# Moving the diagonal key blocks to ScalarE and the probability copies off VectorE in a row-pipelined attention stage

## The chip, the cores and the metric

The kernel runs on one core of a Trainium2 chip. The metric is the device time of the whole program in microseconds, median of several executions. Five engines work in parallel, each on an instruction stream of its own that it executes strictly in order: TensorE (PE: matmuls and transposes), VectorE (DVE), ScalarE (ACT), GpSimd (POOL) and SyncE (SP, which issues transfers). They meet only in semaphores: an instruction may add to one when it is done, and an engine may wait until one has reached a number. Everything behind a waiting instruction on the same engine waits with it.

## The reference

Eight layers on x of shape (8, 128, 256): four attentions, each followed by a feed-forward part. The change touches the second pair. What is computed there, cut to what matters:

```python
x = x + L1_xattn(layernorm(x), ctx)      # 16 heads of 16, T = 128 rows against 128 keys, 8 batch rows
    q = rms_norm(x @ Wq + bq, gq);  k = rms_norm(ctx @ Wk_img + bk_img, gk_img);  v = ctx @ Wv_img + bv_img
    out = softmax(q k^T / 4) v  @ Wo + bo
x = x + L1_ffn(layernorm(x))             # 256 -> 1024 -> 256, 4-bit fake-quantised
    h = relu(x_q @ W1_q^T + b1_q);  h_q = clip(round(h / s2), 0, 15) * s2;  out = h_q @ W2_q^T + b2_q
```

Every batch row (128 x 256) is independent of the others here, which is what the kernel pipelines over.

## The kernel before

The program is one long hand-written schedule. Each engine's part of a stage is a Python function, and the stage of the change is `s23_pe`, `s23_act`, `s23_dve` and `s23_pool` (lines 1331 to 1753). The order in which an engine's calls are written is its order on the chip; nothing reorders it.

A batch row's attention is done in two halves h = 2n and 2n + 1 of eight heads each. `WINDOWS` runs w from -4 to 15, and every engine makes its share of window w before that of w + 1. With k, odd = divmod(w, 2), the even and the odd window of "row k" hold, beside the softmax work of half w, pieces of other batch rows: the projections and the RMS norm of row k + 2, the residual and layer norm of row k - 1, and the feed-forward of rows k - 2 and k - 3. The functions that the prediction follows, with the line of the instruction:

- PE: `scores(w + 1)` L1376, `turn_probs(w)` L1383 (transposes the probabilities), then in an even window `output` L1406, `down(k - 3)` L1442, `project_context(k + 2)` L1340, `project_rows(k + 2)` L1346, `up(k - 2, 0)` L1434, and in an odd one `turn_rows` L1419, `turn(k + 2)` L1361, `up(k - 2, 1)` L1434; last in each window `weigh(w)` L1398 (probabilities times values).
- ACT: `copy_probs` L1485, `exps` L1493, `squares` L1504 (sums of squares for the RMS norm), `copy_rows` L1518, `copy_qk` L1512, `relu` L1527.
- DVE: `maxima` L1590, `normalise` L1581, `divide` L1603 and L1607, `copy_probs` L1597, `add` L1620, `feed` L1637 and L1640, the layer-norm statistics L126 to L130, `apply` L134, `bias` L1564, `values` L1571, `quantise` L1626 and L1630.
- POOL: `ln_rsqrt` L139, `rms` L1686 and L1689, `bias` L1702, `diagonal` L1696, `quantise` L1706 to L1712.

`diagonal` builds c_kb, in which the keys of each head stand in rows of their own with zeros elsewhere, by multiplying the 128 x 128 key block with the four columns of a 0/1 mask `hm`; `scores` needs it. The transposed probabilities of one half lie in two PSUM banks of 512 columns; ACT copies the first bank and DVE the second, each with a semaphore (`c_PT`, `c_PTv`), and `weigh` waits for both. After the last `weigh` PE goes on with the next layer's projections (L1919), issued behind it in the same stream.

Of the kernel before, what the change touches and what calls it, by code (L numbers as in the profile page):

```python
# [25 lines left out]
ALU = mybir.AluOpType  # L26
# [5 lines left out]
KD = D // 128  # L32
# [39 lines left out]
def build(nc, x, ctx, ctxT, mask, maskT, kvmask, a_wqT, a_wkT, a_wvT, a_bq, a_bk, a_bv, a_sel,  # L72
# [5 lines left out]
    with ex:  # L78
# [1252 lines left out]
        def s23_pe(pe):  # L1331
# [32 lines left out]
            def scores(h):  # L1364
                n, c = divmod(h, 2)
                pe.wait_ge(c_qkT, n + 1)
                pe.wait_ge(c_kbd, h + 1)
                if h == 1:
                    pe.wait_ge(c_qkT, 2)
                    pe.wait_ge(c_v, 2)  # L1370
                if h >= 2:
                    pe.wait_ge(c_PT, h - 1)
                    pe.wait_ge(c_PTv, h - 1)
                for i in range(2):
                    half = slice(64 * i, 64 * i + 64)
                    t = pe.matmul(P[:, 2 + 2 * c + i, :], c_qT[n % 2][half, c, :], c_kb[n % 2][half, c], start=True,  # L1376
                                  stop=True)
                t.then_inc(c_s, 1)
# [8 lines left out]
            def weigh(h):  # L1387
                n, c = divmod(h, 2)
                pe.wait_ge(c_PT, h + 1)
                pe.wait_ge(c_PTv, h + 1)  # L1390
                pe.wait_ge(c_v, n + 1)
                if c == 0 and n > 0:
                    pe.wait_ge(c_x, n)
                for what in range(2):
                    for i in range(2):
                        for r in range(4):
                            j = 2 * r + i
                            t = pe.matmul(P[32 * r:32 * r + 32, 6, c * D + what * T:c * D + what * T + T],  # L1398
                                          c_one[:, i, :] if what else c_vp[n % 3][:, 8 * c + j, :],
                                          c_pt[h % 2][:, j, :], start=(i == 0), stop=(i == 1))  # L1400
                t.then_inc(c_pv, 1)
# [47 lines left out]
            for w in WINDOWS:  # L1449
                k, odd = divmod(w, 2)  # L1450
                if 0 <= w + 1 < HALVES:
                    scores(w + 1)
                if 0 <= w < HALVES:
                    turn_probs(w)
                if not odd:
                    if 0 <= k - 1 < B:
                        output(k - 1)
                    if 0 <= k - 3 < B:
                        down(k - 3)
                    if 2 <= k + 2 < B:  # L1460
                        project_context(k + 2)
                        project_rows(k + 2)
                    elif k == -2:
                        project_rows(0)
                else:
                    if 0 <= k - 1 < B:
                        turn_rows(k, 1)
                    if 0 <= k + 2 < B:
                        turn(k + 2)
                    if k == -2:  # L1470
                        project_rows(1)
                if 0 <= k - 2 < B:
                    up(k - 2, odd)
                if 0 <= w < HALVES:
                    weigh(w)
                if 1 <= w + 5 < B:
                    turn_routed(w + 5)
            return output, turn_rows, up, down

        def s23_act(act):  # L1480
            def copy_probs(h):
                act.wait_ge(c_t, h + 1)
                if h >= 2:
                    act.wait_ge(c_pv, h - 1)
                act.activation(c_pt[h % 2][:, 0:4, :].rearrange("p j t -> p (j t)"), P[:, 2 + 2 * (h % 2), :],  # L1485
                               ACT.Copy).then_inc(c_PT, 1)

            def exps(h):
                act.wait_ge(c_mx, h + 1)
# [17 lines left out]
            def copy_qk(n):  # L1507
                act.wait_ge(c_tr, n + 1)
                if n >= 2:
                    act.wait_ge(c_s, 2 * n - 2)  # L1510
                    act.wait_ge(c_kbd, 2 * n - 2)
                act.activation(c_qT[n % 2].rearrange("p j t -> p (j t)"), P[:, QK_BANK[n], :], ACT.Copy).then_inc(c_qkT, 1)  # L1512

            def copy_rows(k, bank):
                act.wait_ge(tb_pe, TURNED[k])
# [22 lines left out]
            for w in WINDOWS:  # L1538
                k, odd = divmod(w, 2)
                if 0 <= w < HALVES:  # L1540
                    copy_probs(w)
                if 0 <= w + 1 < HALVES:
                    exps(w + 1)
                if not odd:
                    if 0 <= k + 2 < B:
                        squares(k + 2)
                else:
                    if 0 <= k - 1 < B:
                        copy_rows(k, 1)
                    if 0 <= k + 2 < B:  # L1550
                        copy_qk(k + 2)
                if 0 <= k - 2 < B:
                    relu(k - 2, odd)
                if 1 <= w + 5 < B:
                    copy_routed(w + 5)
            return copy_rows, relu

        def s23_dve(dve):
# [26 lines left out]
            def maxima(h):  # L1585
                dve.wait_ge(c_s, h + 1)
                if h >= 2:
# [1 line left out]
                bank = 2 + 2 * (h % 2)  # L1589
                dve.tensor_reduce(c_m[h % 2], P[:, bank:bank + 2, :].rearrange("p a (j t) -> p (a j) t", t=T), AX.X,  # L1590
                                  ALU.max, negate=True).then_inc(c_mx, 1)

            def copy_probs(h):
                dve.wait_ge(c_t, h + 1)
                if h >= 2:
                    dve.wait_ge(c_pv, h - 1)
                dve.tensor_copy(c_pt[h % 2][:, 4:8, :].rearrange("p j t -> p (j t)"),  # L1597
                                P[:, 3 + 2 * (h % 2), :]).then_inc(c_PTv, 1)

            def divide(h):  # L1600
                n, c = divmod(h, 2)
# [46 lines left out]
            for w in WINDOWS:  # L1648
                k, odd = divmod(w, 2)
                if 0 <= w + 1 < HALVES:  # L1650
                    maxima(w + 1)
                if odd and 0 <= k + 2 < B:
                    normalise(k + 2)
                if odd and 0 <= w - 1 < HALVES:
                    divide(w - 1)
                if 0 <= w < HALVES:
                    copy_probs(w)
                if not odd:
                    if 0 <= k - 1 < B:
                        add(k - 1)  # L1660
                    if 0 <= k - 3 < B:
                        feed(k - 3)
                    if 0 <= k - 1 < B:
                        apply("attend", k - 1)
                    if 0 <= k - 3 < B:
                        apply("feed", k - 3)
                    if 0 <= k + 2 < B:
                        bias(k + 2)
                        values(k + 2)
                else:  # L1670
                    if 0 <= k - 2 < B:
                        quantise(k - 2, 0)
                    if 0 <= w < HALVES:
                        divide(w)
                    if 0 <= k - 2 < B:
                        quantise(k - 2, 1)
                if 2 <= w + 6 < B:
                    routed_row(dve, w + 6)
            return add, quantise, feed, apply

        def s23_pool(pool):
            def rms(n):
# [4 lines left out]
                    c_ve, 1)  # L1687
                pool.wait_ge(c_ve, n + 1)
                pool.tensor_tensor(c_rst[:, n % 2, :], c_vet[:, n % 2, :], mhalf[:, 0:2], ALU.pow).then_inc(c_rs, 1)  # L1689

            def diagonal(n):
                pool.wait_ge(c_qkT, n + 1)
                for c in range(KD):
                    if n >= 2:
                        pool.wait_ge(c_s, 2 * n - 3 + c)
                    pool.tensor_tensor(c_kb[n % 2][:, c], c_qT[n % 2][:, 2 + c:3 + c, :].broadcast_to([128, 4, T]),  # L1696
                                       hm.rearrange("p (j a) -> p j a", a=1).broadcast_to([128, 4, T]),
                                       ALU.mult).then_inc(c_kbd, 1)

            def bias(n):  # L1700
                pool.wait_ge(xn_ready, 2 * B + n + 1)
                pool.tensor_tensor(X[:, n, :], X[:, n, :], cbo, ALU.add).then_inc(c_cb, 1)  # L1702
# [26 lines left out]
            for w in WINDOWS:  # L1729
                k, odd = divmod(w, 2)  # L1730
                if odd and 2 <= w + 6 < B:
                    routed(w + 6)
                if not odd:
                    if 0 <= k - 1 < B:
                        ln_rsqrt(pool, LN_FIRST + 2 * B + LN23["attend", k - 1], LN23["attend", k - 1] % 2)
                    if 0 <= k - 3 < B:
                        ln_rsqrt(pool, LN_FIRST + 2 * B + LN23["feed", k - 3], LN23["feed", k - 3] % 2)
                    if 0 <= k + 2 < B:
                        rms(k + 2)
                    if 2 <= w + 6 < B:  # L1740
                        routed(w + 6)
                else:
                    if 0 <= k < B:
                        bias(k)
                    if 0 <= k + 2 < B:
                        diagonal(k + 2)
                    if 0 <= k - 1 < B:
                        quantise(k - 1)
            for what in (("attend", B - 1), ("feed", B - 3)):
# [1403 lines left out]
```

## Time and profile before

| | |
|---|---|
| time, median of 3 runs | 1213.58 us (1206.4 to 1214.52) |
| the profiled execution: its own time | 1215.49 us |
| its span in the trace | 1213.5 us |
| busy: PE / DVE / ACT / POOL | 1058.6 / 717.7 / 502.6 / 319.9 us |
| the stage of the change, first `exps` to last `weigh` | 441.53 to 563.00 us, 121.47 us |
| busy in it: PE / DVE / ACT / POOL | 98.99 / 96.24 / 73.45 / 54.59 us |

Times inside the program are microseconds from the start of the span. In the row lists below a line reads: start, length, engine, source line, operation, tensors written and read, count. Neighbouring instructions of the same kind are merged into one line; the brackets give idle time ahead of it and what ended that. Because instructions of one engine overlap a little, the distance from one start to the next is the price of an instruction in a full queue, and its length is what somebody who waits for its result sees. "issue" means that the releaser of a wait is not visible.

### The profile page before, as it was taken

The numbers are of one execution on the slowest core, as the hardware profiler recorded it, in microseconds if no ns is written. First come the engines' busy times: TensorE is split into PE (matmuls) and PEld (weight loads), VectorE is DVE, ScalarE is ACT, GpSimd is POOL, SyncE is SP. The second block draws the span as 40 slices with busy tenths as digits, with TensorE's granted clock in tenths as the row PEclk, the third lists the DMA queues.
The fourth block names the chain that finished last, engine by engine and source line by source line (L and its number), as shares of the span: only waits on it lengthen the run. The fifth ranks groups of instructions, "written<-read, shape, count | busy, mean of one in ns | idle before, by whom it ended". The sixth has DMA issues, their size and how long they took to land.

```text
span 1213.5 us, 20040 instructions
## 1 busy us (share of the span) xinstructions
PE 1058.6 (87%) x6826; PEld 803.0 (66%) x6826; DVE 717.7 (59%) x1700; ACT 502.6 (41%) x1785; POOL 319.9 (26%) x440
## 2 busy tenths in 40 slices
PE   6898788699999868878999999999789999996694
PEld 3665555489999745656878777776556666664472
DVE  5576775711222276887656565566677777775544
ACT  2255557233333144665433334243445555554120
POOL 6252331112332233553100000001212222220572
PEclk9899999689999968989999999999999999999797
DMA  6764442689888406100111101122000000000795
GB/s 194 268 209 143 142 133 81 240 314 331 317 329 321 141 26 227 52 1 31 36 55 36 36 1 36 35 88 88 1 1 5 5 5 6 6 5 13 223 312 180
DMA packets 85218, 141.72 MB, mean 117 GB/s; under 512 B 10090, under 2 KB 58490, under 8 KB 79202
## 3 DMA queue, kind: packets, MB, share of 16 engines
q1 hardware_dynamic: 71193, 116.84, 29.1%
q0 software_dynamic: 4416, 12.06, 2.9%
q10 hardware_dynamic: 9508, 11.55, 2.8%
q8 instruction: 55, 0.90, 0.3%
q14 instruction: 46, 0.37, 0.1%
HBM read 117.51 MB, written 22.72 MB: 116 GB/s over the span
## 4 chain that ended last, share of the span: by engine, by line
PE 60%; DVE 12%; DMA 9%; issue 7%; ACT 4%; SPq 4%; POOL 3%; DVEq 0%; POOLq 0%; ACTq 0%
PE P L968 6%; PE P L978 6%; PE P L1928 4%; PE P L1968 4%; PE P L2114 4%; PE P L2061 4%; DMA scr_qk<-big 3%; PE P L1919 3%; PE P L2880 2%; PE P L2067 2%; PE P L2103 2%; PE P L2089 2%; DMA big<-placed 2%; PE P L2897 1%; PE P L1940 1%
## 5 line engine op out<-in xcount | busy, mean ns | idle before, releaser
L139 POOL TENSOR_TENSOR lrs<-lve,mhalf 128x1 f32<-128x1 f32 x64 | 36.6, 572 | 328.3 <-DVE lve L130 284.2
L576 DVE TENSOR_REDUCE small<-P 128x2 f32<-128x512 f32 x128 | 84.2, 683 | 44.4 <-PE P L403 44.4
L1009 ACT ACTIVATE big<-P,big 128x128 f32<-128x128 f32 x184 | 52.4, 368 | 124.5 <-PE P L968 124.5
L2255 ACT ACTIVATE big<-P,small 128x128 f32<-128x128 f32 x128 | 45.2, 366 | 128.4 <-DVE small L2438 128.4
L656 ACT ACTIVATE big<-P 128x512 f32<-128x512 f32 x128 | 73.6, 599 | 59.0 <-PE P L423 52.0
L968 PE MATMUL P<-big 128*128 128x128 f32 x736 | 87.5, 278 | 0.6 <-DMA big<-b_w 0.5
L968 PEld LDWEIGHTS P<-big 128*128 128x128 f32 x736 | 85.6, 195 | 1.1 <-DMA big<-b_w 1.1
L1111 DVE COPY big<-P 128x256 f32<-128x256 f32 x23 | 9.8, 425 | 125.9 <-PE P L978 125.9
L978 PE MATMUL P<-big 128*128 128x256 f32 x368 | 83.1, 379 | 0.0
L271 PE MATMUL P<-CT,big 128*128 128x256 f32 (+1 forms) x224 | 69.7, 441 | 5.7 <-ACT big L248 4.4
L978 PEld LDWEIGHTS P<-big 128*128 128x128 f32 x368 | 68.2, 190 | 8.4
L403 PE MATMUL P<-big 90*128 90x256 bf16 x256 | 51.1, 282 | 13.8 <-DVE small L576 12.2
L1919 PE MATMUL P<-XNT,big 128*128 128x128 f32 x512 | 62.6, 275 | 0.0
L2114 PE MATMUL P<-big 128*128 128x256 f32 x256 | 61.8, 385 | 0.4 <-DVE big L2635 0.4
L2356 ACT ACTIVATE big<-P 128x512 f32<-128x512 f32 x32 | 19.1, 597 | 102.5 <-PE P L2067 102.5
L2061 PE MATMUL P<-big,XNT 128*128 128x512 f32 x128 | 60.4, 594 | 1.1 <-DVE big L2579 1.1
L1968 PE MATMUL P<-big 128*128 128x256 f32 x256 | 60.6, 380 | 0.0
L1928 PE MATMUL P<-big,CT 128*128 128x512 f32 x128 | 60.1, 592 | 0.0
L1919 PEld LDWEIGHTS P<-XNT,big 128*128 128x128 f32 x512 | 59.7, 192 | 0.2 <-issue 0.2
L2347 ACT ACTIVATE big<-P,small 128x128 f32<-128x128 f32 x128 | 56.7, 459 | 5.2 <-DVE small L2624 5.2
L2429 DVE COPY big<-P 128x512 f32<-128x512 f32 x32 | 22.1, 691 | 60.5 <-PE P L1928 60.4
L1152 POOL DMA_INDIRECT moe_y<-big x23 | 25.0, 1089 | 122.3 <-DVE big L1111 122.3
(387 smaller groups left out, 2530.8 us busy)
## 6 DMA issues: line engine op xcount, KB each, us to landing
big<-b_w SPq DMA_DIRECT2D x23, 1028.0 KB
big<-b_w SPq DMA_DIRECT2D x23, 1024.0 KB
big<-scr_qk SPq DMA_DIRECT2D x96, 96.0 KB
big<-keys_t SPq DMA_DIRECT2D x8, 1024.0 KB, 6.4
big<-i_wgu SPq DMA_DIRECT2D x23, 352.0 KB
keys_t<-XNT ACTq DMA_DIRECT2D x24, 256.0 KB, 2.1
big<-moe_y SPq DMA_DIRECT2D x16, 256.0 KB, 4.3
big<-i_wd SPq DMA_DIRECT2D x23, 176.0 KB
```

Source lines behind the costliest of these rows:

```text
L271: t = pe.matmul(P[:, key_bank(p), lo:hi], k_wts[:, g, k, 128 * j:128 * j + 128], CT[:, k, 512 * r + lo:512 * r + hi], start=(k == 0), stop ...
L576: dve.tensor_reduce(negM[:, h, :], P[:, h % 2, :].rearrange("p (c s) -> p c s", c=2), AX.X, ALU.max, negate=True).then_inc(a_max, 1)
L656: act.activation(ER[:, g % 8], P[:, second_bank(i), :].rearrange("p (c t) -> p c t", c=2), ACT.Exp).then_inc(a_e, 1)
L968: m = pe.matmul(P[:, 2 * (j % 2) + f // 4, f % 4 * 128:f % 4 * 128 + 128], w1x[j % 3][:, k * F0 + f * 128:k * F0 + f * 128 + 128], xgT[j % ...
L978: m = pe.matmul(P[:, 6 + j % 2, 0:D], hT[j % 2][:, f, :], w2x[j % 3][:, f, :], start=(f == 0), stop=(f == FC - 1))
L1009: act.activation(hT[j % 2][:, f, :], P[:, 2 * (j % 2) + f // 4, f % 4 * 128:f % 4 * 128 + 128], ACT.Gelu_apprx_tanh, bias=w1x[j % 3][:, 2 ...
L1919: t = pe.matmul(P[:, 0, j * T:j * T + T], e_wqs[:, g, k, j * 128:j * 128 + 128], XNT[:, k, b * T:b * T + T], start=(k == 0), stop=(k == KD ...
L1928: t = pe.matmul(P[:, 2, :], CT[:, k, b * T:b * T + T], e_wvs[:, g, k, :], start=(k == 0), stop=(k == KD - 1))
L1968: t = pe.matmul(P[:, 7, 0:D], e_o[:, j, :], e_wos[:, 4 * g + j, :], start=(g == 0 and j == 0), stop=(g == 3 and j == 3))
L2061: t = pe.matmul(P[:, 0, :], XNT[:, k, b * T:b * T + T], h_wqs[:, g, k, :], start=(k == 0), stop=(k == KD - 1))
L2114: t = pe.matmul(P[:, 7, 0:D], h_o[:, j, :], h_wos[:, 4 * g + j, :], start=(g == 0 and j == 0), stop=(g == 3 and j == 3))
L2347: t = act.activation(h_pr[m % 2][:, j, :], P[:, 4 - 2 * (m % 2), j * T:j * T + T], ACT.Exp, bias=h_bi[m % 2][:, j:j + 1], scale=h_rq[:, m ...
```

## The change

1. `diagonal` moves from POOL to ACT: where POOL used one 128 x 512 multiplication for each half (two for each batch row), ACT uses four copies of 128 x 128 with a per-partition scale `hm[:, j:j + 1]` (eight for each batch row). It stands right behind `copy_qk`, which now goes ahead of `copy_rows`.
2. ACT's `copy_probs` copies both PSUM banks in one instruction of 1024 columns, and DVE's is gone. `weigh(h)` now waits for `c_o >= h`, that is for `divide(h - 1)`, where it waited for `c_PTv`.
3. DVE's `bias` stands ahead of the two `apply` calls, where it stood behind them.
4. ACT's `relu(k - 2, 0)` stands ahead of `squares(k + 2)`, where it stood behind; `relu(k - 2, 1)` stays behind the copies of its window.
5. PE's `up(k - 2, 1)` stands ahead of `turn(k + 2)`, where it stood behind.

The diff, cut to its core:

```diff
 PE      if h >= 2:
             pe.wait_ge(c_PT, h - 1)
-            pe.wait_ge(c_PTv, h - 1)
...
         def weigh(h):
             pe.wait_ge(c_PT, h + 1)
-            pe.wait_ge(c_PTv, h + 1)
+            if h > 0:
+                pe.wait_ge(c_o, h)
...
             if 0 <= k - 1 < B:
                 turn_rows(k, 1)
+            if 0 <= k - 2 < B:
+                up(k - 2, 1)
             if 0 <= k + 2 < B:
                 turn(k + 2)
...
-        if 0 <= k - 2 < B:
-            up(k - 2, odd)
+        if not odd and 0 <= k - 2 < B:
+            up(k - 2, 0)
...
 ACT     copy_probs(h):
-        act.activation(c_pt[h % 2][:, 0:4, :].rearrange("p j t -> p (j t)"), P[:, 2 + 2 * (h % 2), :],
-                       ACT.Copy).then_inc(c_PT, 1)
+        bank = 2 + 2 * (h % 2)
+        act.activation(c_pt[h % 2].rearrange("p j t -> p (j t)"),
+                       P[:, bank:bank + 2, :].rearrange("p a n -> p (a n)"), ACT.Copy).then_inc(c_PT, 1)
...
+    def diagonal(n):
+        act.wait_ge(c_qkT, n + 1)
+        for c in range(KD):
+            if n >= 2:
+                act.wait_ge(c_s, 2 * n - 3 + c)
+            for j in range(4):
+                t = act.activation(c_kb[n % 2][:, c, j, :], c_qT[n % 2][:, 2 + c, :], ACT.Copy,
+                                   scale=hm[:, j:j + 1])
+            t.then_inc(c_kbd, 1)
...
         if not odd:
+            if 0 <= k - 2 < B:
+                relu(k - 2, 0)
             if 0 <= k + 2 < B:
                 squares(k + 2)
         else:
+            if 0 <= k + 2 < B:
+                copy_qk(k + 2)
+                diagonal(k + 2)
             if 0 <= k - 1 < B:
                 copy_rows(k, 1)
-            if 0 <= k + 2 < B:
-                copy_qk(k + 2)
-        if 0 <= k - 2 < B:
-            relu(k - 2, odd)
+            if 0 <= k - 2 < B:
+                relu(k - 2, 1)
...
 DVE     (copy_probs(h) and its call are gone)
         if not odd:
             if 0 <= k - 1 < B:
                 add(k - 1)
             if 0 <= k - 3 < B:
                 feed(k - 3)
+            if 0 <= k + 2 < B:
+                bias(k + 2)
             if 0 <= k - 1 < B:
                 apply("attend", k - 1)
             if 0 <= k - 3 < B:
                 apply("feed", k - 3)
             if 0 <= k + 2 < B:
-                bias(k + 2)
                 values(k + 2)
...
 POOL    (diagonal(n) and its call are gone)
```

How the streams stand now. ScalarE, from the second `exps` of row 2 through row 3: L1493 is `exps`, L1504 `squares`, L1527 `relu`, L1485 `copy_probs`, L1518 `copy_rows`, L1512 `copy_qk`. Before:

```order
220 L1493 ACTIVATE big<-P,small 128x128 x8
221 L1518 ACTIVATE XNT<-P 128x2x128 x2
222 L1512 ACTIVATE big<-P 128x512
223 L1527 ACTIVATE big<-P,small 128x128 x4
224 L1485 ACTIVATE big<-P 128x512
225 L1493 ACTIVATE big<-P,small 128x128 x8
226 L1504 ACTIVATE big,small<-big 128x256 x2
227 L1527 ACTIVATE big<-P,small 128x128 x4
228 L1485 ACTIVATE big<-P 128x512
```

And ScalarE now, where L1496 is `exps`, L1515 `copy_qk`, L1523 the new `diagonal`, L1531 `copy_rows`, L1540 `relu`, L1488 `copy_probs`, L1507 `squares`:

```order
225 L1496 ACTIVATE big<-P,small 128x128 x8
226 L1515 ACTIVATE big<-P 128x512
227 L1523 ACTIVATE big<-big,small 128x128 x8
228 L1531 ACTIVATE XNT<-P 128x2x128 x2
229 L1540 ACTIVATE big<-P,small 128x128 x4
230 L1488 ACTIVATE big<-P 128x1024
231 L1496 ACTIVATE big<-P,small 128x128 x8
232 L1540 ACTIVATE big<-P,small 128x128 x4
233 L1507 ACTIVATE big,small<-big 128x256 x2
234 L1488 ACTIVATE big<-P 128x1024
```

Eleven instructions (one `copy_qk`, eight `diagonal`, two `copy_rows`) now stand between the odd window's `exps` and its `relu` where three stood, and the even window's `relu` has changed places with `squares`.

VectorE at the end of the even window of row 3, where L1637 and L1640 are `feed`, L134 the two `apply`, L1564 `bias`, L1571 `values` and L1590 the next `maxima`. Before:

```order
444 L1640 TENSOR_TENSOR X<-X,big 128x256
445 L126 BN_STATS lstat<-X 128x6
446 L128 BN_AGGR lmv<-lstat 128x2
447 L130 TENSOR_SCALAR lve<-lmv 128x1
448 L134 TENSOR_SCALAR XN<-X,lmv,lrs 128x256 x2
449 L1564 TENSOR_TENSOR big<-P,big 128x512
450 L1571 TENSOR_TENSOR big<-P,big 128x8x16 x2
```

And VectorE at that place now, where L1649 is `feed` and L1580 `bias`:

```order
437 L1649 TENSOR_TENSOR X<-X,big 128x256
438 L126 BN_STATS lstat<-X 128x6
439 L128 BN_AGGR lmv<-lstat 128x2
440 L130 TENSOR_SCALAR lve<-lmv 128x1
441 L1580 TENSOR_TENSOR big<-P,big 128x512
442 L134 TENSOR_SCALAR XN<-X,lmv,lrs 128x256 x2
```

`bias` has moved ahead of both `apply` instructions, and the copy L1597 that stood behind `maxima` and behind `divide` is gone from the stream.

## Rows read from the trace of the kernel before

**Rows 1.** Windows of core 0: length, then busy time of each engine, granted clock.
```profile
499.42:514.79 15.37, 12.71 (x139) 9.63 (x138) 13.59 (x30) 10.05 (x34) 7.97 (x10) 1.00 0.01 2
514.79:531.11 16.32, 13.53 (x135) 10.01 (x134) 13.44 (x29) 10.37 (x36) 7.97 (x10) 0.90 0.01 2
```

**Rows 2.** Timeline of VectorE, one batch row (k = 3 to k = 4).
```profile
499.42 1.21 DVE L1590 TENSOR_REDUCE small<-P 128x8 f32<-128x1024 f32 x1
501.15 1.33 DVE L1581 SCALAR_TENSOR_TENSOR big<-big,small 128x256 f32<-128x256 f32 x2 [0.52 <-POOL small L1689]
502.40 0.94 DVE L1603 RECIPROCAL big<-P 128x128 f32<-128x128 f32 x1
...
503.59 0.68 DVE L1597 COPY big<-P 128x512 f32<-128x512 f32 x1
504.19 0.42 DVE L1626 TENSOR_SCALAR big<-big 128x512 f32<-128x512 f32 x1
504.64 0.43 DVE L1630 TENSOR_SCALAR big<-big 128x512 bf16<-128x512 f32 x1
505.51 0.96 DVE L1603 RECIPROCAL big<-P 128x128 f32<-128x128 f32 x1 [0.45 <-PE P L1398]
...
506.71 0.71 DVE L1626 TENSOR_SCALAR big<-big 128x512 f32<-128x512 f32 x1
507.96 1.22 DVE L1590 TENSOR_REDUCE small<-P 128x8 f32<-128x1024 f32 x1
...
513.46 0.41 DVE L134 TENSOR_SCALAR XN<-X,lmv,lrs 128x256 f32<-128x256 f32 x1 [0.44 <-POOL lrs L139]
513.79 0.68 DVE L1564 TENSOR_TENSOR big<-P,big 128x512 f32<-128x512 f32 x1
```

**Rows 3.** Timeline of TensorE in the same batch row.
```profile
502.54 0.66 PE L1361 MATMUL P<-idf,big 128*128 128x128 f32 x4 [1.93 <-DVE big L1581]
504.37 1.08 PE L1398 MATMUL P<-big 128*32 128x128 f32 x32 [0.73 <-issue]
...
508.24 1.04 PE L1442 MATMUL P<-big 128*128 128x256 bf16 x8
509.11 1.89 PE L1340 MATMUL P<-big,CT 128*128 128x256 f32 x8
...
511.70 0.61 PE L1434 MATMUL P<-big 128*128 128x128 bf16 x8
512.25 1.08 PE L1398 MATMUL P<-big 128*32 128x128 f32 x32
...
514.32 1.09 PE L1383 MATMUL P<-idf,big 128*128 128x128 f32 x8
```

**Rows 4.** Timeline of ScalarE in the same batch row.
```profile
499.14 0.42 ACT L1504 ACTIVATE big<-big 128x256 f32<-128x256 f32 x1 [3.11 <-DVE big L1564]
...
499.96 1.48 ACT L1527 ACTIVATE big<-P,small 128x128 f32<-128x128 f32 x4
501.32 0.60 ACT L1485 ACTIVATE big<-P 128x512 f32<-128x512 f32 x1
501.80 2.19 ACT L1493 ACTIVATE big<-P,small 128x128 f32<-128x128 f32 x8
503.79 0.74 ACT L1518 ACTIVATE XNT<-P 128x256 f32<-128x256 f32 x2
504.32 0.70 ACT L1512 ACTIVATE big<-P 128x512 f32<-128x512 f32 x1
504.80 1.62 ACT L1527 ACTIVATE big<-P,small 128x128 f32<-128x128 f32 x4
```

**Rows 5.** Timeline of GpSimd in the same batch row.
```profile
505.10 2.04 POOL L1696 TENSOR_TENSOR big<-big,small 128x512 f32<-128x512 f32 x2 [3.29 <-ACT big L1512]
507.24 1.20 POOL L1706 TENSOR_SCALAR big<-XNT,small 128x256 f32<-128x256 f32 x1
```

**Rows 6.** Timeline of TensorE: the next batch row's `weigh`.
```profile
519.74 1.94 PE L1398 MATMUL P<-big 128*32 128x128 f32 x32 [0.73 <-issue]
```

More of the change, by code:

```diff
@@ L1591, in maxima @@
                                   ALU.max, negate=True).then_inc(c_mx, 1)
[L1593 to L1598, printed above, removed]
             def divide(h):
@@ L1655, in s23_dve @@
                     divide(w - 1)
-                if 0 <= w < HALVES:
-                    copy_probs(w)
                 if not odd:
@@ L1689, in rms @@
                 pool.tensor_tensor(c_rst[:, n % 2, :], c_vet[:, n % 2, :], mhalf[:, 0:2], ALU.pow).then_inc(c_rs, 1)
[L1691 to L1698, printed above, removed]
             def bias(n):
@@ L1744, in s23_pool @@
                         bias(k)
-                    if 0 <= k + 2 < B:
-                        diagonal(k + 2)
                     if 0 <= k - 1 < B:
```

## The prediction

> **What bounds the kernel now.** The table of windows comes first. One batch row takes 15.37 us at full clock and 16.32 us in the next, where the granted clock averages 0.90 [rows 1]. In those 15.37 us DVE is busy 13.59, PE 12.71, ACT 10.05 and POOL 7.97 us. No engine is full, but DVE is nearest, and busy lengths of neighbours overlap, so the timelines decide.
>
> Read VectorE's next [rows 2]. It stands still three times for another engine: 0.52 us at `normalise` for POOL's reciprocal roots, 0.45 us at the second `divide` for `weigh`, 0.44 us at `apply` for POOL. All else is its own queue. Then TensorE [rows 3]: it stands 1.93 us at `turn` for `normalise` and 0.73 us at `weigh`, whose releaser the view calls "issue". By the code it is DVE's copy: L1597 starts at 503.59 and lasts 0.68, so it ends at 504.27, and `weigh` starts at 504.37 [rows 2, 3]. So in this stage the row's time is set by DVE, with short excursions through `bias`, `squares`, `rms`, `normalise` and through `weigh`. Behind the stage PE goes on in the same stream, so what PE's last `weigh` gains or loses the kernel gains or loses.
>
> **The change part by part.** I price an instruction by the distance between starts where it sits in a full queue, and by its length where somebody waits for it; a handover between engines costs about 0.05 us.
>
> DVE's copy goes: 504.19 - 503.59 = 0.60 us, twice in a batch row, 1.20 us [rows 2]. Moving `bias` ahead of the two `apply` costs nothing on DVE and covers the 0.44 us wait, since `bias` is 0.68 us long [rows 2]. The wait that `weigh` gets in place of the removed one (`divide(h - 1)`) was already implied by DVE's order and ends 0.60 us earlier than the copy did.
>
> ACT takes the work. The eight `exps` run from 501.80 to 503.79, 0.25 us each [rows 4]. Like them a `diagonal` piece is 128 x 128 with one per-partition operand, so I take 8 x 0.25 = 2.0 us. Bounds: two per-partition operands, as in `relu`, cost (501.32 - 499.96) / 4 = 0.34 us, or 2.7 us in all; with none, a 512-column copy takes 0.48 and a 256-column one (504.32 - 503.79) / 2 = 0.265, and that line reaches 0.16 at 128 columns, or 1.3 us [rows 4]. The row nearest in shape and operands is `exps`. `diagonal` also waits for the end of `copy_qk`, so that one costs its length of 0.70 instead of 0.48. The copy of both banks costs 0.48 + 2 x 0.215 = 0.91 us on the same line, 0.43 more than half of it.
>
> A page states a price for such instructions. The Trainium skill (ScalarE: Activation LUTs, What ACT_TABLE_LOAD costs) gives 186 ns plus 0.833 ns a column, 93 ns more for each per-partition operand and 93 ns of overlap; an estimate from it is 8 x 0.293 = 2.3 us for `diagonal`, which would put the sum of this part about 1.2 us higher. The `exps` rows, at 0.25 us, lie under its figure, and I stay with them.
>
> POOL loses 2.04 us that nobody waited long for [rows 5]. That hides nothing: `scores` uses these blocks most of a batch row later. Its `quantise` now waits for the later `copy_rows`, still in time for `up` one row later.
>
> Now the placement, which I think decides. In the odd window `relu(k - 2, 1)` runs from 504.80 to 506.42 and DVE takes its result at 506.71, so it has 0.29 us to spare [rows 2, 4]. After the change `diagonal` (2.0), the longer `copy_qk` (0.22) and the wider copy (0.43) stand ahead of it: 2.65 us, less 0.29, is 2.35 us late. Behind this `relu` queue DVE's `quantise(k - 2, 1)`, the next `maxima` and `add`, and on PE `down(k - 2)` of the next window with both projections, `up`, `weigh` and `scores` behind it. With PE's late work the ACT queue is fed late, and the circle closes. Round it once, at full clock:
>
> - `relu` 1.5 and handover 0.05;
> - `quantise`, 506.71 to 507.96, 1.25 us beside GpSimd's work (0.88 alone, 504.19 to 505.07), and 0.05 [rows 2];
> - PE from the start of `down` at 508.24 through projections, `up`, `weigh`, `scores` to the end of `turn_probs` at 515.41: 7.17 us, and 0.05 [rows 3];
> - ACT: copy 0.91, `exps` 1.99, `copy_qk` 0.70, `diagonal` 2.0, `copy_rows` 0.53.
>
> That is 16.2 us, or 15.8 with the faster `quantise`, against 15.37 now: 0.5 to 0.85 us more for each round. `relu(., 1)` and `diagonal` meet in the odd windows of k = 2 to 5, so there are three rounds.
>
> What a page says bears on that 1.25. The second `quantise` takes 0.71 for the first of its two instructions while POOL's L1696 runs (505.10 to 507.14), the first one 0.42 with POOL idle [rows 2, 5]. The Trainium skill (GPSIMD Engine Reference, 8. Key points) has POOL share its SBUF interfaces with VectorE and slow two-port and two-input instructions; the trace agrees. POOL's L1696 goes, but POOL's L1706, 1.20 us, is released by `copy_rows` just ahead of `relu` and so lies beside this `quantise` again, and I expect no relief.
>
> The sum, to the path of PE's last `weigh`: rows k = 0 and 1, where no `relu` runs, gain the copy ahead of `weigh` (0.60) and up to 0.9 more from the even window's copy and the earlier `bias`, 1.2 to 3.0 for both, I take -2.0. Row 2 enters the circle: +2.35. Three rounds: +1.5 to +2.5, I take +2.0. In rows 6 and 7 there is no `diagonal`; DVE's copies leave the path (-0.6 each of four) and the wider copies enter it where ACT is late (+0.43 each), between -2.4 and +1.7, I take -0.5. Total about +2 us. The profiled execution took 1215.49 us, 2 us more than its span for what lies around it, so it would come to 1217.4. It lies 1.9 above the median, and the same sum on the median of 1213.58 gives 1215.5. With both ends of `diagonal`'s price (+-0.7 a row in four rows) and of the other terms the forecast case spans about -4 to +8, so 1209.5 to 1221.5.
>
> **The rivals.** *DVE's relief wins.* Should the odd `relu` not be late (pieces nearer 0.16 us, and ACT reaching `copy_qk` before PE's `turn` is done), the next circle runs through `normalise` 1.25, `divide` 1.19, handover 0.05, PE from `weigh` at 504.37 to the end of `up` at 512.31, 7.94, handover 0.05, `relu` 1.36, then `squares` and `rms` to `normalise` 2.0 (499.14 to 501.15) [rows 2 to 4]. That is 13.85 us, 1.5 less than now. Four rows give -6, the first two -2, the last two -1: 1204.6. For it speaks that ACT is busy only 10.05 of 15.37 us [rows 1]; against it, that its slack lies in the even window, and the additions in the odd one.
>
> *The clock.* Slower than before. PE stands 1.93 + 0.73 us in a batch row now, and that row kept full clock; the next one, with the same pauses, fell to an average of 0.90, `weigh` took 1.94 in place of 1.08 us and the row 0.95 us more [rows 1, 3, 6]. After the change PE would have a further pause, at `down`: `turn_probs` and `output` are done 3.9 us after `weigh` starts (504.37 to 508.24), but the circle releases `down` some 2.3 us after that. If that pause makes the grant fall to 1.2 GHz in each of six rows, what follows is `down`, the projections and `up`, all on the circle: 0.95 to 1.7 us a row, 6 to 10 us, on top of +2: 1221.5 to 1225.5, say 1224. It decides from about one fall in each row; the trace shows one in two.
>
> That the change doesn't do what it says is excluded by the instruction orders: all five moves are in them.
>
> **How the numbers follow.** Forecast case 0.68, 1215.5 us. DVE's relief 0.14, 1204.6. The clock 0.18, 1224. One per cent, about what a measurement of this kernel can tell from no change, is 12.1 us: 1201.5 to 1225.7. The relief case passes it less than half the time (0.06), the clock case about half the time (0.10), the forecast's own ends about 0.01 each. So 0.07 faster, 0.82 within, 0.11 slower. The range reaches from the better half of the relief case to the upper end of the clock case, 1206 to 1225.5, and leaves out about 2 in 10.
>
> **What the profile after would show.** Right: `quantise` of the odd window waiting 2 us or more for ACT's `relu`; PE waiting about as long at `down` for that `quantise`; no "issue" wait of 0.7 us at `weigh` with DVE behind it, but some wait for `divide`; `diagonal` pieces of 0.25 us from start to start; ACT busy near 14 us in each row; rows 3 to 5 at 15.8 to 16.2 us each; the first rows shorter than now. Wrong: DVE without a wait at the odd `quantise` and rows near 14 us (relief); granted clock under 0.9 over the stage (clock). The forecast would fail above all if ACT's queue has room that I don't see, if `diagonal` from SBUF costs something else than `exps` from PSUM, or if the late stages, which I hold unchanged, start in another alignment.

## The result, and the profile after

The changed kernel is slower: 1220.57 us against 1214.14 us, medians of 17 runs each, ratio 1.0052 with a 95% interval of 1.0036 to 1.0068, that is +6.3 us (4.4 to 8.3). That is the slower side of "no change" within one per cent. One of the 17 runs of the kernel before took 1895.58 us and is left out of the ratio.

The windows view of the changed kernel, two batch rows cut from the `weigh` of one even window to the next (length, busy time of PE, PE's weight loads, DVE, ACT and POOL, granted clock), answers to [rows 1]:

```profile
492.39:510.37 17.98, 14.43 (x139) 10.56 (x137) 12.52 (x27) 13.34 (x41) 6.40 (x9) 0.91 0.00 1
510.37:526.67 16.30, 12.75 (x138) 9.40 (x137) 11.93 (x27) 13.34 (x41) 5.30 (x7) 1.00 0.00 1
```

The first of them has a stretch at 1.2 GHz in it. At full clock a batch row takes 16.30 us where it took 15.37. DVE is busy 1.66 us less than in [rows 1], ACT 3.29 us more (13.34 against 10.05). No engine is busy for the whole row, and yet the row is longer, so look at who waits. VectorE's timeline in the changed kernel (L1635 and L1639 `quantise`, L1606 `maxima`), answering to [rows 2]:

```profile
503.61 0.43 DVE L1635 TENSOR_SCALAR big<-big 128x512 f32<-128x512 f32 x1 [2.65 <-ACT big L1540]
504.07 0.55 DVE L1639 TENSOR_SCALAR big<-big 128x512 bf16<-128x512 f32 x1
504.54 1.21 DVE L1606 TENSOR_REDUCE small<-P 128x8 f32<-128x1024 f32 x1
```

Where there was no wait for ACT, `quantise` of the odd window now stands 2.65 us for `relu`. ScalarE's timeline shows what stands ahead of that `relu` (L1496 `exps`, L1515 `copy_qk`, L1523 `diagonal`, L1531 `copy_rows`, L1540 `relu`, L1488 the copy of both banks), answering to [rows 4]:

```profile
495.59 1.02 ACT L1488 ACTIVATE big<-P 128x1024 f32<-128x1024 f32 x1 [0.79 <-PE P L1382]
496.51 2.17 ACT L1496 ACTIVATE big<-P,small 128x128 f32<-128x128 f32 x8
498.51 0.66 ACT L1515 ACTIVATE big<-P 128x512 f32<-128x512 f32 x1
499.21 2.45 ACT L1523 ACTIVATE big<-big,small 128x128 f32<-128x128 f32 x8
501.56 0.63 ACT L1531 ACTIVATE XNT<-P 128x256 f32<-128x256 f32 x2
502.09 1.49 ACT L1540 ACTIVATE big<-P,small 128x128 f32<-128x128 f32 x4
```

The eight pieces go from 499.21 to 501.56, 2.35 us or 0.294 each, more than the 0.25 of the `exps`. And TensorE's timeline shows where the delay goes on (L1361 `turn`, L1398 `weigh`, L1442 `down`), answering to [rows 3]:

```profile
515.27 0.66 PE L1361 MATMUL P<-idf,big 128*128 128x128 f32 x4 [0.85 <-DVE big L1597]
516.51 1.08 PE L1398 MATMUL P<-big 128*32 128x128 f32 x32 [0.58 <-issue]
...
522.65 1.05 PE L1442 MATMUL P<-big 128*128 128x256 bf16 x8 [2.12 <-DVE big L1639]
```

The wait at `turn` has shrunk from 1.93 to 0.85 us, the one at `weigh` from 0.73 to 0.58, and a new one of 2.12 us stands at `down` for the odd window's `quantise`. The releaser that the view doesn't see at `weigh` is `divide` by the code: it ends at 516.41 (L1616, 516.12, 0.29 us long), and `weigh` starts 0.10 us later, as it started 0.10 us behind VectorE's copy before. Both old waits are cheaper and the row is still longer: everything that follows in PE's stream (both projections, `up`, the next `weigh`) is queued behind `down`.

Behind the stage nothing differs in these two traces. From the next layer's first projection (562.9 us in the trace before, 562.7 in this one) to the first `up` matmul of the last layer's experts it is 573.2 and 573.5 us. What lies ahead of the stage and in the last layer varies by several us from one execution to the next, so a single trace's span says little here: this one's is 1212.7 us, less than the 1213.5 of the kernel before. I therefore measure the stage, from the first `exps` to that projection.

The stage has a lead-in ahead of the first `exps`, the windows w = -4 to -1, and the change is in it too: `diagonal` of the first two batch rows now stands in ScalarE's queue ahead of the copies that TensorE's next transposes wait for. One such pair of transposes, before and after:

```profile
437.44 0.41 PE L1355 MATMUL P<-idf,XN 128*128 128x128 f32 x2 [0.56 <-ACT XNT L1533]
```

```profile
433.66 0.66 PE L1355 MATMUL P<-idf,XN 128*128 128x128 f32 x2 [1.39 <-ACT XNT L1546]
```

From the stage's first `project_context` to its first `exps` it is 26.2 us in this trace of the kernel before and 27.3 in that of the changed one.

### The profile page after: what moved, and what is told of

Same layout as the page of the kernel before. It is cut to its first block, busy times and chain, and to the rows that moved or that the text cites. A ratio compares the mean times of both kernels' runs of the same rounds, so it can differ in the third digit from the quotient of the medians.

```text
span 1212.7 us, 20044 instructions
## 1 busy us (share of the span) xinstructions
PE 1057.1 (87%) x6826; PEld 801.4 (66%) x6826; DVE 706.8 (58%) x1684; ACT 529.1 (44%) x1849; POOL 303.7 (25%) x424
## 4 chain that ended last, share of the span: by engine, by line
PE 63%; DVE 11%; DMA 7%; ACT 7%; issue 5%; POOL 3%; SPq 3%; ACTq 0%; DVEq 0%; POOLq 0%
PE P L968 7%; PE P L978 7%; PE P L1925 4%; PE P L1965 4%; PE P L2111 4%; PE P L2058 4%; PE P L1916 3%; PE P L2877 2%; PE P L2064 2%; DMA scr_qk<-big 2%; PE P L2100 2%; PE P L2086 2%; PE P L2894 1%; PE P L1937 1%; DMA big<-placed 1%
## 5 line engine op out<-in xcount | busy, mean ns | idle before, releaser
L656 ACT ACTIVATE big<-P 128x512 f32<-128x512 f32 x128 | 73.6, 599 | 54.2 <-PE P L423 46.8
L1152 POOL DMA_INDIRECT moe_y<-big x23 | 25.0, 1089 | 121.4 <-DVE big L1111 121.4
```

The costliest lines, as they stand in the source:

```text
L656: act.activation(ER[:, g % 8], P[:, second_bank(i), :].rearrange("p (c t) -> p c t", c=2), ACT.Exp).then_inc(a_e, 1)
```

## Experiments

**The two kernels again: how much is the clock?** The timed difference is 6.3 us, the stage in the first two traces differs by 125.1 - 121.4 = 3.7 us. Both kernels were profiled twice more, without an edit.

> The kernel before, profiled once more, to see how far the stretches of 1.2 GHz differ from one execution to the next. The timed difference of the change is +6.4 us, the stage (first exps to the next layer's first projection) in the two traces differs by 3.7 only. If chance in the clock explains the rest, this stage comes out shorter than the 121.4 us of the first trace, 117 to 120 us, with less time at 1.2 GHz. If it repeats 121.4 us, the difference is elsewhere.

> The kernel before a third time, for the same question: 117 to 122 us for the stage; the clock's stretches after the same pauses of TensorE, but not all of them each time.

> The changed kernel, profiled once more. Theory A: the full rows repeat at 16.3 us at full clock, and the stage takes 122 to 126 us, against 125.1 in its first trace. Clock theory: the time at 1.2 GHz is larger than in the kernel before in both its traces.

> The changed kernel a third time: 122 to 126 us for the stage, full rows at full clock 16.3 us.

The four executions took 1217.33 and 1216.54 us (before) and 1220.83 and 1219.45 us (changed); a further one of the kernel before beside them, without a trace, took 1213.20. The second trace of the kernel before has a stage of 120.6 us, a little over the 117 to 120 expected; the other three lie where they were expected. The stage, cut at the starts of `weigh` (there are 16; the fifth and sixth are in row 2, where the first `relu` and the late `diagonal` meet), in us:

| stretch | before, three traces | changed, three traces | difference of means |
|---|---|---|---|
| lead-in, first `project_context` to first `exps` | 26.2, 26.2, 26.2 | 27.3, 27.2, 27.2 | +1.0 |
| whole stage | 121.4, 120.6, 118.6 | 125.1, 125.5, 123.8 | +4.6 |
| 1st to 5th `weigh` (rows 0, 1) | 32.5, 31.0, 30.4 | 29.4, 29.3, 27.8 | -2.5 |
| 5th to 7th (row 2) | 14.0, 14.0, 14.0 | 16.3, 18.0, 16.3 | +2.9 |
| 7th to 13th (three rounds) | 46.7, 47.2, 46.8 | 50.3, 50.3, 50.0 | +3.3 |
| 13th to 16th (rows 6, 7) | 18.2, 16.9, 17.0 | 19.0, 17.3, 18.7 | +0.9 |
| mean granted clock in the stage | 0.91, 0.92, 0.93 | 0.91, 0.92, 0.93 | 0 |
| the same in rows 0 and 1 | 0.84, 0.94, 0.94 | 0.94, 0.94, 1.00 | |
| in row 2 | 1.00, 1.00, 1.00 | 1.00, 0.91, 1.00 | |
| in the three rounds | 0.96, 0.93, 0.93 | 0.93, 0.96, 0.96 | |
| in rows 6 and 7 | 0.92, 1.00, 1.00 | 0.82, 0.93, 0.83 | |

The windows view of one row at full clock in the third trace of the kernel before and in the second of the changed one:

```profile
489.52:504.75 15.23, 12.57 (x136) 9.48 (x137) 13.46 (x29) 9.94 (x35) 7.98 (x10) 1.00 0.25 65
```

```profile
499.63:515.92 16.29, 12.76 (x139) 9.41 (x137) 11.94 (x27) 13.31 (x41) 5.28 (x7) 1.00 0.00 1
```

So the rows repeat to 0.15 us where the clock is full (15.23 and 15.37 before, 16.29 and 16.30 changed), unless they follow a slow stretch: behind a row of 18.06 us the second trace of the kernel before has one of 13.94. One fall of the clock costs a row of the changed kernel 1.7 us (row 2 took 18.0 in one trace, 16.3 in the others). Both kernels have the same mean clock in their three traces, and a row at full clock is 1 us longer all the same, so the clock isn't what makes the changed kernel slower. It does move the single terms: it fell in rows 0 and 1 above all before, and in rows 6 and 7 after the change. At full clock rows 0 and 1 take 14.93 + 14.29 us before (each row from another trace) and 27.8 after, -1.5; row 2 is +2.3; rows 6 and 7 take 16.9 before and 16.2 in e5 and e8 (below), which have the changed kernel's order there, -0.8. With the rounds, +3.3 at about the same mean clock on either side, the four add up to +3.3, which leaves, as an estimate, 1.3 of the 4.6 us to the clock. Whether those falls come with the change or by chance three traces can't tell. The stage with its lead-in gives +5.7 us, inside the timed interval of 4.4 to 8.3.

Experiments e1 to e8 were timed beside new runs of the kernel before, with a median of 1221.96 us for e1 to e4 and 1222.01 us for e5 to e8, so only ratios compare with the times above. The ratios are those on record; the quotient of the two medians differs from them a little (0.991 for e2, where the ratio is 0.9935).

**e1: `relu` ahead of the diagonal pieces.** On the changed kernel, ScalarE only:

```diff
             else:
+                if 0 <= k - 2 < B:
+                    relu(k - 2, 1)
                 if 0 <= k + 2 < B:
                     copy_qk(k + 2)
                     diagonal(k + 2)
                 if 0 <= k - 1 < B:
                     copy_rows(k, 1)
-                if 0 <= k - 2 < B:
-                    relu(k - 2, 1)
```

> The changed kernel, with one move on ScalarE: the odd window's relu stands right behind exps, ahead of copy_qk, diagonal and copy_rows. Same instructions, same counts. Theory A (late relu: the diagonal pieces push relu, and with it quantise, down and the projections, 2.3 to 2.7 us late in each full row): the waits of 2.65 us at quantise and 2.1 us at down go, rows 3 to 5 take about 15 us, and the kernel gains 3 to 5 us on the changed one, ratio to before 0.998 to 1.002. Theory B (the clock: more pauses of TensorE make the grant fall more often): TensorE still pauses at turn, and the time stays within 1.5 us of the changed kernel. Theory C (ScalarE simply has too much work, wherever relu stands): same as B, no gain.

Measured: ratio to before 1.0005 (0.9982 to 1.0028), stage 117.2 us. The interval does not overlap that of the changed kernel (1.0036 to 1.0068). ACT's work is the same, so it is not its amount (theory C) but its place that costs. The waits at `quantise` and `down` are gone; a row at full clock, between two odd `weigh`:

```profile
499.18:514.22 15.04, 12.98 (x136) 9.39 (x137) 12.23 (x27) 13.22 (x43) 5.89 (x8) 1.00 0.01 2
```

It isn't down to 14 us, and the traces show the diagonal pieces ahead of `copy_rows`, whose result TensorE's `project_context` and GpSimd wait for. TensorE's timeline of this kernel, then GpSimd's:

```profile
504.38 1.97 PE L1340 MATMUL P<-big,CT 128*128 128x256 f32 x8 [0.30 <-ACT XNT L1531]
...
507.53 0.62 PE L1434 MATMUL P<-big 128*128 128x128 bf16 x8 [0.33 <-POOL big L1711]
```

```profile
504.07 1.15 POOL L1705 TENSOR_SCALAR big<-XNT,small 128x256 f32<-128x256 f32 x1 [6.86 <-ACT XNT L1531]
```

In both places tried in this odd window the pieces make somebody late: `relu` or `copy_rows`, and through GpSimd's `quantise` the next `up`. The prediction held that handover to be in time; it is in the changed kernel, and no longer here.

**e2: the diagonal back on GpSimd.** All other moves kept:

```diff
-            def diagonal(n):          # in s23_act, and its call
+            def diagonal(n):          # in s23_pool, as before the change
```

> The changed kernel with diagonal back on GpSimd as one multiplication a half (1.04 us each), all other moves kept. Theory A: the price of the change is the diagonal pieces ahead of relu (2.35 us a row), so this one loses the waits and keeps the relief of VectorE: rows near 14 us, 6 to 9 us under before, ratio 0.993 to 0.995. Theory B (clock): no more than 2 us under before. If the wide copy or the new order of relu and squares was what cost, the time stays over before.

Measured: 1211.16 us against 1221.96, ratio 0.9935 (0.9912 to 0.9958), stage 111.5 us. The row:

```profile
495.29:509.30 14.01, 12.58 (x137) 9.49 (x138) 12.26 (x27) 11.01 (x35) 7.84 (x10) 1.00 0.01 3
```

14.01 us is what the circle of the "DVE's relief" rival was worked out to take, 13.85. VectorE's timeline of this kernel has `quantise` (here L1624) almost without a wait:

```profile
511.91 0.43 DVE L1624 TENSOR_SCALAR big<-big 128x512 f32<-128x512 f32 x1 [0.19 <-ACT big L1530]
```

So the other moves together are worth about 0.65% to the good, and the diagonal's move costs 1.2% (1.0052 against 0.9935).

**e3: the diagonal alone, on the kernel before.**

```diff
 ACT odd window:  copy_rows(k, 1); copy_qk(k + 2)
+                 diagonal(k + 2)         # eight copies with a scale
                  relu(k - 2, 1)
 POOL:
-                 diagonal(k + 2)
```

> The kernel before with only the diagonal moved: eight ScalarE copies of 0.29 us behind copy_qk, nothing on GpSimd; probability copies, bias, relu and up stay where they were. Theory A: relu of the odd window is 2.4 us later and all of it falls on the path, since VectorE keeps its copies: 6 to 10 us over before, ratio 1.005 to 1.008, more than the whole change costs. Theory C' (the diagonal is hidden in ScalarE's idle time, since it is idle 5 us a row): no more than 1 us over before.

Measured: ratio 1.0072 (1.0054 to 1.0089), 1229.71 against 1221.96 us. VectorE's and TensorE's timelines in this kernel, in a row at full clock:

```profile
527.00 0.43 DVE L1637 TENSOR_SCALAR big<-big 128x512 f32<-128x512 f32 x1 [2.12 <-ACT big L1537]
```

```profile
527.94 1.05 PE L1442 MATMUL P<-big 128*128 128x256 bf16 x8 [1.46 <-DVE big L1641]
```

The waits at `quantise` and `down` are there without any of the other moves, and shorter than in the changed kernel (2.65 and 2.12), since DVE with its copies arrives later. The rows at full clock take 15.5 and 15.9 us. The stage (125.0 us) has the lowest clock of all traces, 0.89, so its length is no measure for the move alone. The timed runs don't free the ratio from this either: over the whole program their mean granted clock is 0.943, against 0.947 of the kernel before beside them, so a part of the 0.72% may be the clock's.

**e4: the wide copy alone, on the kernel before.**

```diff
-    act: c_pt[:, 0:4] <- P[bank]         dve: c_pt[:, 4:8] <- P[bank + 1]
+    act: c_pt <- P[bank:bank + 2]
 weigh(h):
-    pe.wait_ge(c_PTv, h + 1)
+    if h > 0: pe.wait_ge(c_o, h)
```

> The kernel before with only the probability copy moved: ScalarE copies both banks in one instruction of 1024 columns, VectorE none, weigh waits for divide(h - 1). Theory A: VectorE loses 1.2 us a row and ScalarE gains 0.85 in idle time, so the kernel is 2 to 4 us faster than before, ratio 0.997 to 0.998. Rival: ScalarE's copy comes later than VectorE's did and weigh waits for it, no gain or up to 2 us slower.

Measured: ratio 0.9977 (0.9956 to 0.9998). The row repeats at 15.2 us (`weigh` at 509.47 and 524.69, against 15.23 before), with a wait of 0.69 us at `quantise`. So 1.20 us less of VectorE's work in each row makes a full row no shorter; the gain lies in the rows without an odd `relu` (row 1 takes 13.5 us in place of 14.3 at full clock). What holds the row is a circle through the late `bias`: ScalarE idles 2.5 us until `bias` is done, then comes `squares` (496.06), the rest of its queue and the odd `relu` to 503.78, then VectorE's queue from `quantise` at 503.81, whose first instruction takes 0.97 us here, and with a wait of 0.44 us at `apply`, to `bias` again at 510.56. VectorE's timeline:

```profile
503.81 0.97 DVE L1620 TENSOR_SCALAR big<-big 128x512 f32<-128x512 f32 x1 [0.69 <-ACT big L1528]
510.23 0.41 DVE L134 TENSOR_SCALAR XN<-X,lmv,lrs 128x256 f32<-128x256 f32 x1 [0.44 <-POOL lrs L139]
```

**e5: half of the diagonal on each engine.** On the changed kernel:

```diff
 ACT   diagonal(n):
-        for c in range(KD):
+        for c in range(1):               # then_inc(c_kbd, 1)
 POOL
+      diagonal(n):  for c in range(1, KD): tensor_tensor(...).then_inc(c_PTv, 1)
 PE    scores:
-        pe.wait_ge(c_kbd, h + 1)
+        pe.wait_ge(c_PTv if c else c_kbd, n + 1)
```

> The changed kernel with half of the diagonal blocks back on GpSimd: ScalarE makes those of the first half (four copies, 1.2 us), GpSimd those of the second (1.04 us), each with a semaphore of its own. Theory A (the pieces ahead of relu are the price, and they add one for one once its slack is gone): relu is 1.2 us earlier than in the changed kernel, rows 3 to 5 near 15.2 us, and the time lies about half way between the changed kernel and the one with the diagonal on GpSimd, ratio to before 0.998 to 1.001. A threshold instead of a slope would put it at one of the two ends, 0.9935 or 1.005.

Measured: ratio 0.997 (0.9953 to 0.9988), just under the 0.998 to 1.001 expected and nearer to e2 than half way, stage 114.7 us, rows of 15.12 us at full clock (`weigh` at 490.64, 505.76 and 520.88). VectorE's and TensorE's waits:

```profile
500.68 0.43 DVE L1636 TENSOR_SCALAR big<-big 128x512 f32<-128x512 f32 x1 [1.49 <-ACT big L1541]
```

```profile
501.74 1.05 PE L1442 MATMUL P<-big 128*128 128x256 bf16 x8 [0.94 <-DVE big L1640]
```

Rows: 14.01, 15.12, 16.30 us for none, half and all of the pieces. That is +1.11 and +1.18 us for 4 x 0.294 = 1.18 us each: one for one, apart from the little slack that the first half finds. A threshold is excluded by the rows.

**e6: `squares` first again.** On the kernel of e2:

```diff
 ACT even window:
-    relu(k - 2, 0); squares(k + 2)
+    squares(k + 2); relu(k - 2, 0)
```

> The kernel of e2 (diagonal on GpSimd, all else as changed) with the even window's relu back behind squares. If the early relu is worth something beyond the moved bias, this is slower than e2 by 1 to 2 us. If squares is what TensorE's turn waits for, having it first gains as much. I expect neither: both must be done before normalise, ratio to before within 0.001 of e2's 0.9935.

Measured: ratio 0.9943 (0.9921 to 0.9966), stage 110.9 us against 111.5, a row at full clock 13.87 in place of 14.00: by time no difference from e2 that these runs can tell.

**e7: `bias` alone, on the kernel before.**

```diff
+    bias(k + 2)
     apply("attend", k - 1); apply("feed", k - 3)
-    bias(k + 2)
     values(k + 2)
```

> The kernel before with only VectorE's bias moved ahead of the two apply calls. It takes the 0.44 us wait for GpSimd out of each row and starts squares and rms about 0.8 us earlier; VectorE still holds its copies. Theory A, in which VectorE's own queue sets the row: 1 to 3 us faster than before, ratio 0.9975 to 0.999. Rival: normalise comes no earlier because of maxima ahead of it, no change.

Measured: ratio 0.9979 (0.9956 to 1.0002), stage 116.9 us against 118.6 to 121.4. By time it points to a gain of 2 to 3 us, but the interval just includes none. The rows are plainer. Two at full clock, from even to even and from odd to odd `weigh`:

```profile
495.60:509.72 14.12, 12.57 (x138) 9.49 (x136) 13.16 (x28) 10.08 (x33) 7.89 (x10) 1.00 0.01 2
501.85:516.10 14.25, 12.57 (x136) 9.48 (x137) 13.39 (x29) 10.07 (x35) 7.89 (x10) 1.00 0.01 3
```

The row is 1.1 us shorter than the 15.23 to 15.37 of the kernel before, with all of VectorE's work still there: of the 1.2 us between 15.2 and the 14.0 of e2, nearly all comes with this one move.

**e8: `up` behind `turn` again.** On the kernel of e2:

```diff
-    up(k - 2, 1); turn(k + 2)
+    turn(k + 2); up(k - 2, 1)
```

> The kernel of e2 with TensorE's up of the odd window back behind turn. Up then runs after turn, 0.55 us between turn and weigh, which waits 0.6 us there anyway. Theory: no change against e2, ratio to before 0.993 to 0.995. Rival: relu of the odd window gets its input 1.5 us later and is late at quantise, 2 to 3 us slower than e2.

Measured: ratio 0.9933 (0.9915 to 0.9951), 1211.27 against 1222.01 us, stage 109.3 us with a mean clock of 0.97. By time the same as e2. These two are the fastest versions found, about 8 us under the kernel before. Over the whole program the timed runs of e2 and e8 have a mean granted clock of 0.950 and 0.951 against 0.947 before, so a part of the 8 us may be the clock's; the rows of 14.0 us at full clock hold without it.

## Why the prediction was right, and where not

It gave 1215.5 us, 2 us over the median of before, in a range of 1206 to 1225.5, and one per cent as the bound of "no change". The measured +0.52% lies inside, on the side that it named. The late `relu` held step by step, and it is what the change costs; that the amount of DVE's work set the row before did not. The sum was too small by about 2.6 us against the stage (+4.6) and 4.3 against the times (+6.3).

- *DVE set the row before, with short excursions:* right only in the excursion. Taking 1.20 us of copies off DVE leaves the full row at 15.2 us (e4); moving `bias` ahead of the two `apply`, which takes no work off it, gives 14.1 to 14.25 (e7). So the row hung on where `bias` stands in DVE's queue, on the path through `bias`, `squares` and what follows them, and not on how much DVE has to do.
- *The odd `relu` is late, `quantise` and `down` wait.* Named at 2 us or more; 2.65 and 2.12 us in the trace. e1, e2 and e5 take the pieces away from in front of it, and the waits go or halve. Shown.
- *Rows 0 and 1 gain 2.0 us:* 2.5 as a mean of three traces, 1.5 at full clock. *Row 2 loses 2.35:* 2.3 at full clock, 2.9 as a mean of three traces.
- *The lead-in:* the sum had no term for it. `diagonal` of the first two batch rows costs 1.0 us there in each of the three traces. It stays at 26.2 and 26.3 us in e7 and e4, which leave `diagonal` on GpSimd, at 26.2 to 26.6 in e2, e6 and e8, which put it back there, and is 27.0 in e3, which moves nothing else.
- *Three rounds cost 2.0 us, each 16.2 at most:* this term was mis-sized. The row is 16.3 and the rounds cost 3.3. Two errors in it nearly cancel in the circle. The diagonal piece costs 0.294 us and not 0.25, +0.35 a row. The Trainium skill (ScalarE: Activation LUTs, What ACT_TABLE_LOAD costs) gave an estimate of 0.293, and the trace agrees. I had preferred the nearest row, and that row reads PSUM where `diagonal` reads SBUF. ScalarE's timeline of the kernel before held the hint: `squares` with 256 columns from SBUF goes on after 0.32 us (499.14 to 499.46), `copy_rows` with 256 from PSUM after 0.265. Further on it has the same instruction with either source, an exponential of 128 x 128 with one per-partition bias and a sum read out behind it, first from PSUM and then from SBUF:

```profile
640.78 0.36 ACT L2255 ACTIVATE big<-P,small 128x128 f32<-128x128 f32 x1
641.03 0.20 ACT L2255 ACTIVATION_READ_ACCUMULATOR big<-P,small 128x1 f32 x1
...
647.98 0.40 ACT L2276 ACTIVATE big<-big,small 128x128 f32<-128x128 f32 x1 [4.79 <-DVE small L2567]
648.28 0.19 ACT L2276 ACTIVATION_READ_ACCUMULATOR big<-big,small 128x1 f32 x1
```

  From PSUM the next instruction starts after 0.25 us, from SBUF after 0.30. The other way, `quantise` takes 0.93 us (503.61 to 504.54) and not 1.25. And having worked out 15.8 to 16.2 for the row, I took the middle of the range for the sum, where the row's own value was its end.
- *Rows 6 and 7 gain 0.5:* they lose 0.9 as a mean of three traces, but there the granted clock of the changed kernel averaged 0.82 to 0.93 in each of them, and that of the kernel before fell in one of three. At full clock it is 16.2 us (e5, e8) against 16.9, a gain of 0.8, so the term stands, and the loss goes with the clock. `weigh` waits for the wide copy itself now, as foreseen, and less than it waited for DVE's copy. TensorE's timeline, before and then changed:

```profile
550.28 1.08 PE L1398 MATMUL P<-big 128*32 128x128 f32 x32 [1.26 <-issue]
...
561.91 1.08 PE L1398 MATMUL P<-big 128*32 128x128 f32 x32 [0.71 <-issue]
```

```profile
549.03 1.08 PE L1398 MATMUL P<-big 128*32 128x128 f32 x32 [0.66 <-ACT big L1488]
...
561.71 1.08 PE L1398 MATMUL P<-big 128*32 128x128 f32 x32 [0.23 <-ACT big L1488]
```

- *No relief from GpSimd's departure:* wrong. The instruction of `quantise` that took 0.71 us beside GpSimd's two-input L1696 [rows 2, 5] takes 0.43 us now, while GpSimd's one-input L1707 (503.26, 1.08 us long) runs beside it. So what slowed this one was that operation, not GpSimd's being busy. The second instruction of `quantise`, which writes bf16, takes 0.55 us beside one-input operations (504.07) and 0.43 without (504.64 in [rows 2]).
- *The clock rival:* mean clock equal in three traces of each kernel, and 0.947 over the whole program in the changed kernel's 17 timed runs as in the runs of the kernel before beside the experiments. It isn't the cause, but by the estimate above it has about 1.3 of the 4.6 us in the traces. *DVE's relief:* not what happened, but its circle of 13.85 us was measured as 14.01 once the pieces were off ACT.

That the circle came out right to 0.1 us was luck in part, since its two errors of 0.35 and 0.32 us cancel. In the sum the missing lead-in, the rounds taken too small and the clock all add, and only the width of the range took them in. What stays open is the last 0.6 us between the +5.7 of the stage with its lead-in and the times' +6.3. The interval covers it. The traced executions themselves differ by 1.8 us only (means of 1216.5 and 1218.3), since what lies ahead of the stage was 2.6 us shorter on average in those of the changed kernel; it varies by 7 us over all traces, whatever the kernel.

## What to carry to other kernels

When work moves to an engine that is idle a third of the time, ask in which window it is idle: ACT had 5 us to spare in each row, but only 0.29 us ahead of the one instruction that two other engines waited for, and every microsecond put in front of it came back as a microsecond of the row. In a pipeline of in-order queues follow each late result around until it comes back to where it started; the length of that circle is the row, and here it was right to 0.2 us for both versions. The same holds for the relief: 1.2 us less work on the busiest engine made a full row no shorter, and one instruction moved up by two places took 1.1 us off it. A bundle of moves should be timed apart: four of these five were worth 8 us together (two of the four, the orders of `relu` and `up`, show nothing by time), and the fifth cost 14.

## What was not expected of the hardware

- A 128 x 128 ScalarE copy with a per-partition scale, SBUF to SBUF, is 0.294 us from start to start; `exps` of the same size with a per-partition bias, from PSUM, is 0.25. One exponential with its sum read out behind it is 0.25 from PSUM and 0.30 from SBUF (641.03 - 640.78 and 648.28 - 647.98 in the kernel before).
- A 128 x 1024 ScalarE copy reading two PSUM banks in one instruction costs 0.92 us from start to start (495.59 to 496.51), on the line through 0.265 for 256 and 0.48 for 512 columns.
- VectorE's 128 x 512 one-input instruction in fp32 took 0.42 us with GpSimd idle, 0.43 beside a one-input GpSimd operation, and 0.71 to 0.97 beside a two-input one. It ended 0.28 us behind the end of that operation both where it began 0.43 us ahead of the end (506.71, before) and where it began 0.69 us ahead (503.81, e4).
- The same pause of TensorE is followed by a fall of the granted clock in one row and not in the next, and in another row in the next execution; one fall costs a row of the changed kernel 1.7 us (18.0 against 16.3).
